# Scaling the exponentials before they are turned, and the projection after the 8-head attention as three fp32r terms

## The reference, cut to what matters

```python
hid = _group_norm(x, norm_w, norm_b)
q, k, v = ...                                  # 8 heads of 32 channels, 196 tokens
weight = einsum('bhct,bhcs->bhts', q * scale, k * scale)
weight = softmax(weight, axis=-1)
a = einsum('bhts,bhcs->bhct', weight, v)
h = einsum('oc,bcl->bol', proj_w, a) + proj_b
return x + h
```

## Time and profile before

| what | value |
|---|---|
| median of 3 runs | 2169.7 us (2168.6 to 2170.22) |
| the profiled execution's own time | 2170.37 us |
| its span (first to last instruction) | 2168.3 us |
| mean granted TensorE clock | 0.976 of full speed |
| PE busy | 2076.3 us (96%) |
| DVE busy | 1820.4 us (84%) |
| ACT busy | 1527.8 us (70%) |
| POOL busy | 1278.3 us (59%) |

### The profile page before, as it was taken

The page is one execution under the profiler, slowest core; times in us unless marked ns, Lnnn a source line. Parts: engine busy times, 40 slices in busy tenths (PEclk is TensorE's granted clock), DMA queues, the critical chain, the costliest instruction groups (busy, mean ns, idle before and its releaser), DMA issues.

```text
span 2168.3 us, 58678 instructions
## 1 busy us (share of the span) xinstructions
PE 2076.3 (96%) x15232; PEld 1686.7 (78%) x15232; DVE 1820.4 (84%) x4359; ACT 1527.8 (70%) x5172; POOL 1278.3 (59%) x2954
## 2 busy tenths in 40 slices
PE   4679999999999999999999999999999999999987
PEld 3466888888888788888878888887888888788775
DVE  6778899988888998988899898888989888887532
ACT  2256777777777777777777777777777777777763
POOL 2455666666666666666666666666666666664311
PEclk8799999999999999999999999999999999999977
DMA  3000011001101100110110011011101100100000
GB/s 126 15 23 23 16 39 39 29 23 37 37 22 37 37 30 22 37 37 22 37 37 30 22 37 37 23 36 37 37 15 37 37 31 28 38 31 24 24 23 23
DMA packets 29828, 70.22 MB, mean 32 GB/s; under 512 B 6261, under 2 KB 7105, under 8 KB 29761
## 3 DMA queue, kind: packets, MB, share of 16 engines
q1 hardware_dynamic: 26928, 67.68, 9.0%
q10 hardware_dynamic: 2832, 1.73, 0.3%
HBM read 30.86 MB, written 12.85 MB: 20 GB/s over the span
## 4 chain that ended last, share of the span: by engine, by line
PE 91%; DVE 3%; POOL 2%; issue 2%; ACT 1%; SPq 1%; DMA 0%; POOLq 0%; DVEq 0%; ACTq 0%
PE ps_c L1166 19%; PE ps_a L1166 17%; PE ps_e L1166 17%; PE ps_b L1166 17%; PE ps_s L1166 10%; PE ps_s L1216 8%; POOL gn_t L579 1%; PE ps_a L1292 1%; DVE y L1158 1%; PE ps_e L1454 0%; PE ps_e L1292 0%; PE ps_b L1454 0%; PE ps_e L1399 0%; SPq L475 0%; ACT e L827 0%
## 5 line engine op out<-in xcount | busy, mean ns | idle before, releaser
L827 ACT ACTIVATE e<-ps_s,nm 98x196 f32<-98x196 f32 x1024 | 426.1, 446 | 89.9 <-DVE nm L956 89.8
L590 POOL TENSOR_SCALAR xn<-x,gn_scale,gn_shift 128x196 f32<-128x196 f32 x384 | 353.2, 933 | 20.8 <-POOL gn_shift L585 20.8
L1158 DVE SCALAR_TENSOR_TENSOR y<-opad,w_dw,y 128x406 f32<-128x406 f32 x512 | 301.8, 645 | 0.0
L1139 DVE SCALAR_TENSOR_TENSOR y<-xpad,w_dw,y 128x406 f32<-128x406 f32 x512 | 300.8, 640 | 0.0
L956 DVE TENSOR_REDUCE nm<-ps_s 98x4 f32<-98x784 f32 x256 | 240.6, 962 | 41.8 <-PE ps_s L1166 41.8
L834 ACT COPY pt<-ps_s 98x392 f32<-98x392 f32 x512 | 229.1, 503 | 42.6 <-PE ps_s L1216 41.8
L568 POOL TENSOR_TENSOR gn_t<-gn_group 128x4 f32<-128x4 f32 x96 | 34.3, 358 | 372.9 <-DVE gn_group L1006 286.5
L827 ACT ACTIVATION_READ_ACCUMULATOR e<-ps_s,nm 98x1 f32 x1024 | 231.6, 226 | 0.0
L1216 PE MATMUL ps_s<-w_eye,e 98*98 98x98 f32 x2048 | 204.6, 251 | 0.6 <-ACT e L827 0.6
L1216 PEld LDWEIGHTS ps_s<-w_eye,e 98*98 98x98 f32 x2048 | 186.3, 131 | 24.1 <-issue 16.2
L581 POOL TENSOR_SCALAR gn_t<-gn_t 128x4 f32<-128x4 f32 x288 | 119.7, 416 | 58.6 <-POOL gn_t L579 58.6
(11 more groups left out here) (245 smaller groups left out, 5596.8 us busy)
## 6 DMA issues: line engine op xcount, KB each, us to landing
x_in<-in_x SPq DMA_DIRECT2D x32, 392.0 KB, 3.1
x_res<-in_x SPq DMA_DIRECT2D x32, 392.0 KB, 3.3
x2b<-x SPq DMA_DIRECT2D x32, 392.0 KB, 2.6
out<-x SPq DMA_DIRECT2D x32, 392.0 KB, 2.6
out_pairs<-out SPq DMA_DIRECT2D x32, 392.0 KB, 3.5
w_q<-in_q SPq DMA_DIRECT2D x3, 256.0 KB
w_k<-in_k SPq DMA_DIRECT2D x3, 256.0 KB
w_v<-in_v SPq DMA_DIRECT2D x3, 256.0 KB
```

The lines of the kernel that those rows point to most:

```text
L590: g.tensor_scalar(dst[:, c, of_image(i)], src[:, c, of_image(i)], t.scale[:, j:j + 1], t.shift[:, j:j + 1], ALU.mult, ALU.add).then_inc(t. ...
L827: s.activation(e2[:, j, tc], tile(use)[0:HALF, of_image(tc)], ACT.Exp, bias=nm2[:, j, tc:tc + 1], accum_out=den2[:, 2 * i + tc, h:h + 1]). ...
L1139: v.scalar_tensor_tensor(out=dst, in0=window(xpad, c, k, CR), scalar=tap, in1=dst, op0=ALU.mult, op1=ALU.add).then_inc(conv1_steps.sem, 1)
L1158: v.scalar_tensor_tensor(out=dst, in0=window(opad, c, k, CR), scalar=tap, in1=dst, op0=ALU.mult, op1=ALU.add).then_inc(conv2_steps.sem, 1)
```

## The change

1. The division moves ahead of the transposes. `rden{g}_{m}` (DVE) takes the reciprocals of the sums of two units as soon as their exponentials are done; a new use `less{g}_{j}` (ACT) multiplies the two 98 x 196 halves of `e2[j]` in place by them; the transposes wait for `p2_done[j]`, which that use counts up. `rden`, `rt`, `rep0`, `rep1` with their copies, their product with `heads` and the multiplication into `an2` are gone.
2. `av{g}` on ACT writes the high part `as2[:, 0]` in fp32r (a copy with a cast), and a new use `av{g}` on DVE subtracts it from PSUM into the low part `as2[:, 1]`. `proj{c}` is a `split_product` of `ws["p2"]` and `as2`. `p2` joins the weights that are split once at the start (two more casts on ACT, two more subtractions on DVE; the cast of `heads` is gone).
3. All five tables and `BANK_USES` are new. The highest lag goes from 5 turns to 6.

```diff
@@ ACT
-                    p = pair_of(t, u, ACT_AT["rt"])
-                    if p is not None:
-                        act.wait_ge(*full(p, "rt"))
...
-                        s.copy(rt2[:, 0], tile("rt")[0:H2, 0:N2]).then_inc(rt_high.sem, 1)
...
+                            p = pair_of(t, u, ACT_AT[f"less{g}_{j}"])
+                            if p is not None:
+                                h = HG * (g % 2) + j
+                                act.wait_ge(rden_done.sem, rden_done.at(p, 2 * g + j // 2 + 1))
+                                for tc in range(2):
+                                    s.activation(e2[:, j, tc], e2[:, j, tc], ACT.Copy,
+                                                 scale=rden2[:, 2 * i + tc, h:h + 1]).then_inc(p2_done[j].sem, 1)
...
-                            s.copy(a2[:, i, g % 2], tile(use)[:, 0:TOK]).then_inc(emptied(use), 1)
+                                act.wait_ge(*full(p - 1, latest("proj0", "proj1")))
+                            s.copy(as2[:, 0, i, g % 2], tile(use)[:, 0:TOK]).then_inc(a2_high.sem, 1)
@@ DVE
-                        v.reciprocal(rden2[:], den2[:]).then_inc(rden_done.sem, 1)
...
-                        v.tensor_tensor(rt2[:, 1], tile("rt")[0:H2, 0:N2], rt2[:, 0], ALU.subtract).then_inc(emptied("rt"), 1)
...
-                            v.tensor_tensor(an2[:, :, c], tile(use)[:, 0:N2].rearrange("p (i n) -> p i n", i=2),
-                                            a2[:, :, c], ALU.mult).then_inc(emptied(use), 1)
+                    for g in range(GROUPS):
+                        i = g // 2
+                        for m in range(2):
+                            p = pair_of(t, u, DVE_AT[f"rden{g}_{m}"])
+                            if p is not None:
+                                for j in (2 * m, 2 * m + 1):
+                                    dve.wait_ge(*read(p, f"sc{g}_{j}"))
+                                h = HG * (g % 2) + 2 * m
+                                v.reciprocal(rden2[:, 2 * i:2 * i + 2, h:h + 2], den2[:, 2 * i:2 * i + 2, h:h + 2]
+                                             ).then_inc(rden_done.sem, 1)
...
+                            dve.wait_ge(a2_high.sem, a2_high.at(p, g + 1))
+                            v.tensor_tensor(as2[:, 1, i, g % 2], tile(use)[:, 0:TOK], as2[:, 0, i, g % 2], ALU.subtract
+                                            ).then_inc(emptied(use), 1)
@@ PE
-                                for source in elsewhere(use, f"sc{g}_{j}"):
-                                    pe.wait_ge(*read(p, source))
+                                pe.wait_ge(p2_done[j].sem, p2_done[j].at(p, 2 * g + 2))
...
-                        for j in range(4):
-                            last = nc.tensor.transpose(tile("rt")[0:H2, j * HALF:(j + 1) * HALF], rden2[:, j],
-                                                       eye[0:HALF, 0:HALF])
...
-                            product(tile(use)[:, 0:N2], lambda k: heads[:, c], lambda k: rt2[:, k]).then_inc(filled(use), 1)
...
-                            product(tile(use)[:, 0:N2], lambda k: w["p2"][:, k, of_chunk(c)], lambda k: an2[:, :, k]
-                                    ).then_inc(filled(use), 1)
+                            split_product(tile(use)[:, 0:N2], lambda a, k: ws["p2"][:, a, k, of_chunk(c)],
+                                          lambda b, k: as2[:, b, :, k]).then_inc(filled(use), 1)
@@ one line of the tables
-    "max2_1": 490, "max3_0": 520, "max3_1": 524, "rden": 535, "rt": 544, "rep0": 561, "rep1": 563, "proj1": 570,
+    "rden2_1": 521, "av1": 524, "max3_0": 536, "max3_1": 539, "rden3_0": 544, "av2": 548, "rden3_1": 553, "av3": 582,
```

More of the change, by code:

```diff
@@ L104 @@
     "qb2": (128, KC), "kb2": (128, KC), "vb2": (128, KC), "p2": (128, KC, CH), "pb2": (128, KC),
-    "heads": (H2, KC, 128), "eye": (128, 128),
+    "eye": (128, 128),
     "gn3_w": (128, 4), "gn3_b": (128, 4), "q3": (128, KC, CH), "k3": (128, KC, CH), "v3": (128, KC, CH),
@@ L114 @@
 W_BY_ACT = ("q0", "k0", "v0", "bias0", "dw2", "o0", "mlp0", "gn1_w", "gn1_b", "group32", "group8", "kvb1", "pb1",
-            "gn2_w", "gn2_b", "kb2", "pb2", "heads", "gn3_w", "gn3_b", "ob3")
-W_EARLY = ("k1", "q1", "v1", "vb1_rep", "p1", "q2", "k2", "v2", "vb2", "q3", "k3", "v3", "o3", "vb3", "qb3_rep")
-SPLIT = {"kv1": 2 * CH, "q1": CH, "q2": CH, "k2": CH, "v2": CH, "v3": CH + 2, "q3": CH}
+            "gn2_w", "gn2_b", "kb2", "pb2", "gn3_w", "gn3_b", "ob3")
+W_EARLY = ("k1", "q1", "v1", "vb1_rep", "p1", "q2", "k2", "v2", "vb2", "q3", "k3", "v3", "o3", "vb3", "qb3_rep",
+           "p2")
+SPLIT = {"p2": CH, "kv1": 2 * CH, "q1": CH, "q2": CH, "k2": CH, "v2": CH, "v3": CH + 2, "q3": CH}
 def build(nc, a):
@@ L358, in build @@
         max2_done = Count("max2_done", UNITS // 2)
-        rden_done = Count("rden_done", 1)
-        rt_high = Count("rt_high", 1)
+        a2_high = Count("a2_high", GROUPS)
+        rden_done = Count("rden_done", 2 * GROUPS)
+        p2_done = [Count(f"p2_done{j}", 2 * GROUPS) for j in range(HG)]
         l3_less_steps = Count("l3_less_steps", 2 * 3)
@@ L444, in early_sources @@
                 yield parts("kv1", k, w["k1"][:, k])
-                for name in ("q1", "q2", "k2", "v2"):
+                for name in ("q1", "q2", "k2", "v2", "p2"):
                     yield parts(name, k, w[name][:, k])
@@ L807, in step @@
                             s.copy(v2[:, i].rearrange("p c n -> p (c n)"), tile(use)[0:HALF, :]).then_inc(emptied(use), 1)
-                    p = pair_of(t, u, ACT_AT["rt"])
-                    if p is not None:
-                        act.wait_ge(*full(p, "rt"))
-                        if has_before(p) and not comes_after("rt", latest("rep0", "rep1")):
-                            act.wait_ge(*full(p - 1, latest("rep0", "rep1")))
-                        s.copy(rt2[:, 0], tile("rt")[0:H2, 0:N2]).then_inc(rt_high.sem, 1)
                     for g in range(GROUPS):
@@ L839, in step @@
                             if has_before(p):
-                                act.wait_ge(*read(p - 1, f"rep{g % 2}"))
-                            s.copy(a2[:, i, g % 2], tile(use)[:, 0:TOK]).then_inc(emptied(use), 1)
+                                act.wait_ge(*full(p - 1, latest("proj0", "proj1")))
+                            s.copy(as2[:, 0, i, g % 2], tile(use)[:, 0:TOK]).then_inc(a2_high.sem, 1)
                     for j in range(4):
@@ L1051, in step @@
                                                    in1=xn1[:, c], op0=ALU.add, op1=ALU.add).then_inc(emptied(use), 1)
-                    p = pair_of(t, u, DVE_AT["rden"])
-                    if p is not None:
-                        for use in ends(*(f"sc{g}_{j}" for g in range(GROUPS) for j in range(HG))):
-                            dve.wait_ge(*read(p, use))
-                        if has_before(p):
-                            dve.wait_ge(*full(p - 1, "rt"))
-                        v.reciprocal(rden2[:], den2[:]).then_inc(rden_done.sem, 1)
@@ L1060, in step @@
-                    p = pair_of(t, u, DVE_AT["rt"])
-                    if p is not None:
-                        dve.wait_ge(rt_high.sem, rt_high.at(p, 1))
-                        v.tensor_tensor(rt2[:, 1], tile("rt")[0:H2, 0:N2], rt2[:, 0], ALU.subtract).then_inc(emptied("rt"), 1)
-                    for c in range(KC):
-                        use = f"rep{c}"
+                    for g in range(GROUPS):
[8 more added lines that the diff above has]
+                                             ).then_inc(rden_done.sem, 1)
+                        use = f"av{g}"
@@ L1066, in step @@
                         p = pair_of(t, u, DVE_AT[use])
                         if p is not None:
-                            dve.wait_ge(*full(p, use))
-                            if has_before(p) and not comes_after(use, latest("proj0", "proj1")):
-                                dve.wait_ge(*full(p - 1, latest("proj0", "proj1")))
-                            for source in ends(f"av{c}", f"av{2 + c}"):
-                                dve.wait_ge(*read(p, source))
-                            v.tensor_tensor(an2[:, :, c], tile(use)[:, 0:N2].rearrange("p (i n) -> p i n", i=2),
-                                            a2[:, :, c], ALU.mult).then_inc(emptied(use), 1)
+                            dve.wait_ge(a2_high.sem, a2_high.at(p, g + 1))
@@ L1392, in step @@
                                ).then_inc(filled(use), 1)
-                    p = pair_of(t, u, PE_AT["rt"])
-                    if p is not None:
-                        pe.wait_ge(*free(p, "rt"))
-                        pe.wait_ge(rden_done.sem, rden_done.at(p, 1))
-                        for j in range(4):
-                            last = nc.tensor.transpose(tile("rt")[0:H2, j * HALF:(j + 1) * HALF], rden2[:, j],
-                                                       eye[0:HALF, 0:HALF])
-                        last.then_inc(filled("rt"), 1)
-                    for c in range(KC):
-                        use = f"rep{c}"
```

(13 more changed lines are left out.)

18 lines of the change are left out of this document (6 added, 12 removed), and 71 rows, old and new, of tables (ACT_AT, BANK_USES, DVE_AT, PE_AT).

## The result

The changed kernel takes **2153.93 us** (median of 4 runs, 2153.33 to 2158.38), the kernel before in the same session 2169.76 us (2168.6 to 2170.22): a ratio of 0.9932, 95% interval 0.9919 to 0.9945. It is faster by 0.7%, some 16 us. Forecast were 2130 us, 1.8% less.

The account below looks back on a forecast made before the run. PE was taken as the bound at 63.06 us a turn; 2170.4 - 28.4 x (63.06 - 61.5) + 5 = 2131.1, less 0.7 for the median, gave 2130 us. Forecast's own range 2110 to 2145, whole range 2108 to 2172.

Parts of the forecast that it names:

- the ends: Time outside the loop's 28.4 turns, 379 us before; the change was to add 5 us, between -5 and +20.
- Saved: 0.34 + 0.54 + 0.35 + 0.20 + 2 x (1.32 - 1.08) = 1.91 us: PE work saved per pair: reciprocal transposes, two heads products, a change of shape, and two fp32 products made fp32r.
- the three terms: Projection on PE: two plain fp32 products of 1.32 us each become six fp32r matmuls at 1.08 us.
- PE not waiting, or by tenths: In the new order, PE's other work covers each group's way from scores to transposes through DVE and ACT.
- The walk: Following both queues' new order through one turn with the pieces' lengths, to find where PE or ACT waits.
- 58.3 + 3.2 = 61.5: ACT's need per turn plus its idle places, in us, taken as the turn; PE's own need was 61.15.
- DVE: DVE's load per turn: +0.9 us from more reciprocals and subtractions, so 57.4 of 61.5 us, not the bound.
- ACT by some tenths: Rival: ACT's uncovered waits are 3.7 to 4.5 us, turn 62.0 to 62.8, 2157 us; chance 0.18.
- open dead time behind the scores: Rival: ACT waits 1.2 us for the maximum in all four groups, turn 63.2, 2179 us; chance 0.13.
- Full duration: Rival: ACT's scalings cost their whole duration, 61.4 + 3.2 = 64.6 us a turn, 2219 us; chance 0.03.
- terms without gain: Rival: the projection's fp32r matmuls run at the fp32 records' rate, turn 62.95, 2172 us; chance 0.02.
- the clock: Rival: TensorE at half clock for a tenth of each turn adds 3 us per pair, 2216 us; chance 0.02.

Follow-up runs that it names:

- e7: e4 without the 32 scalings per pair, so the exponentials are not divided: 2124.83 us, a turn of 61.52.
- e8: e4 with the projection as two plain fp32 products of the high copy, the low part subtracted but unused: 2152.31 us.
- e4: The changed kernel with the moves of e2 and e3 together: 2138.47 us, a turn of 61.74.
- e2: The changed kernel with sum0_1 in DVE_AT moved from 172 to 177, behind the low parts: 2143.65 us.
- e11: The changed kernel with GpSimd's multiplication probs1 in POOL_AT moved from 96 to 113: 2159.64 us.
- e3: The changed kernel with ACT's input activations bn0 and bn1 moved ahead of the copy of q0_0: 2149.41 us.
- e1: The changed kernel without its 32 scalings per pair, so the exponentials are never divided: 2136.04 us, a turn of 61.99.
- e5: The change's work put into the tables and order of the kernel before: 2719.66 us, a turn of 81.89.
- a third move: e4 with gn1 moved behind the last convolution steps, PE_AT 304 to 309 and DVE_AT 307 to 309: 2138.81 us.

## Why the prediction was wrong

The direction and the ends were right, and that PE is the bound before. The gain per turn was 0.75 us instead of 1.56, and the loop's 28.4 turns carry all of the miss: 28.4 x (62.31 - 61.5) = 23 us of the 24 between 2130 and 2154. Two steps failed, by 0.37 and 0.44 us a turn. By the prediction's own steps:

- **"Saved: 0.34 + 0.54 + 0.35 + 0.20 + 2 x (1.32 - 1.08) = 1.91 us": this term failed by 0.37.** It measured 1.54. The first `heads` product was taken with the change of shape ahead of it (0.54 for two records of 174 ns; the second, 0.35, holds none), and the 0.20 behind them was added. But the time beyond equal matmuls is 4.39 us a turn before and 4.39 in e7, in which I find no wait: the total of those costs did not fall with the four records. That they all stand elsewhere now is read from the sum; I haven't traced each one. The arithmetic of the three terms was right: forecast 0.48 us, and e8 against e4 gives 0.52.
- **"PE not waiting, or by tenths": this step failed in size, and it is the larger part.** It allowed 0.35 us (61.5 - 61.15), as ACT's idle places; PE waits 0.79, in two places: 0.47 for `hk0` and 0.31 for `tn2`. The walk followed scores, maxima, exponentials, scalings and transposes, but not the neighbours that the new order had put side by side. The low part of `hk0` runs beside GpSimd's multiplication and then takes 1.21 us instead of 0.55. e2 and e11 remove this wait, and each brings another in its place, of 0.22 us ahead of `gn1` and of 0.54 ahead of `t0_1`. e3 removes the 0.31 of `tn2` behind `bn1` and brings none.
- **"58.3 + 3.2 = 61.5": right in kind, wrong as the bound.** ACT needs 57.33 and is idle 5.0 of 62.3 us, where 58.3 and 3.2 were forecast (the three places named for the 3.2 add up to 3.1). The scalings' distance (0.35) and the places of the idle time were as forecast, but adding idle time to need made ACT the pace setter. e1 takes 10 us off ACT and gets 0.32 us a turn, as much as one small move.
- **DVE** was forecast at 57.4 and is at 56.73: no bound.
- **The ends** were forecast at +5 and are +5.4. That it is so close is luck, as executions of one kernel differ by more. Only the largest term was tested: the 9 us for the scalings where nothing covers them show in e1 (383 to 373) and in e7 against e4 (386 to 378).
- **Rivals.** "ACT by some tenths" had the time (2157, a turn of 62.0 to 62.8) but not the mechanism, as e1 shows. The open dead time behind the scores is there in one of four groups (1.41 us), not in four. Full duration, terms without gain and the clock are excluded by the 0.35, by e8 and by the 1.00 of the window. The granted clock of a turn is lower only in e5 (0.90), where PE is idle 11.4 us of it.

## What to carry to other kernels

When a small product is removed from a full queue, count the distance between its starts and not the piece in the chain: here the cost of changing shape, summed over the turn, stayed. When a timetable is redone, don't only follow the path of the changed work. For each transfer between engines, look at what the other engines do in the same microsecond, and re-price it with the neighbours it now has: here 0.47 us of wait a turn hung on one such pair and 0.31 on one activation put into a full stretch of ACT instead of an idle one, and moving these two was worth as much as the whole change. When a wait goes and the turn gains less than the wait was long, look for the one that came in its place: here 0.47 us went and 0.22 came, and a third move only carried those 0.22 to another place.

## What the runs showed of the hardware

A subtraction of 128 x 392 on DVE, from two tiles in SBUF, took 554 ns alone and 1208 ns when it met a multiplication of 98 x 392 on GpSimd, which itself took 1.09 us instead of 0.84. The tile's view of the changed kernel (durations as minimum, median, maximum in ns):

```profile
L1086 DVE TENSOR_TENSOR xs<-xn,xs x2: 554/881/1208, 1064.2 to 1064.6; 128x392 fp32r<-128x392 f32 x2
```

The second subtraction starts at 1064.6 and the multiplication ends at 1064.33 + 1.09 = 1065.42. The subtraction ends 0.43 us after that, and the multiplication's own excess of 0.25 us is less than what the first subtraction still had to run when it started (1064.33 to 1064.72). So the two seem to have run one behind the other rather than both slower side by side. The Trainium skill ("SBUF — State Buffer", section "SBUF: two separate sides") says that a VectorE operation with two SBUF inputs and a GpSimd operation that reads SBUF take an exclusive lock on a shared pair of ports, so that the loser blocks for the whole instruction. With that the traces agree: the excess of 0.65 us vanishes in e11, where it is DVE's convolution step (line 1133) that runs beside the multiplication and takes 0.95 us instead of some 0.64.

The kernel before shows it more sharply. There the same multiplication meets a product of 128 x 4 on DVE, which lasts 164 ns by its median over the span and 0.71 us here:

```profile
1008.86 0.84 POOL L602 TENSOR_TENSOR p<-s,r 98x392 f32<-98x392 f32 x1
...
1009.01 0.71 DVE L943 TENSOR_TENSOR gn_sq<-gn_mine 128x4 f32<-128x4 f32 x1
```

In 26 turns of that kernel the small product starts 42 to 167 ns behind the multiplication and ends 14 to 18 ns behind its end, each time. So what the later one pays here is what is left of the other engine's instruction when it starts, and that can appear or vanish with a change of the timetable that touches neither operation.
